# A graph layer in steps of 15 tiles instead of 16: second lookup in halves, sums of two spans in turn, slots on the full array

## The reference

```
msg = relu(x[src] + edge_attr)                  # (400000, 32)
agg = segment_sum(msg, dst, 12500)
h   = (1 + eps) * x + agg
y   = x + h @ W.T + b
out = (y - mean(y)) / sqrt(var(y) + 1e-5)       # over the 32 features
```

## Time and profile before

| what | value |
|---|---|
| median of 3 executions | 2076.12 us (2075.43 to 2078.41) |
| span of the profiled execution | 2071.9 us |
| PE busy | 2016.0 us, 97% |
| DVE busy | 1648.3 us, 80% |
| ACT busy | 1565.9 us, 76% |
| POOL busy | 1519.9 us, 73% |
| full steps | 195 |

### The profile page before, as it was taken

The page is one execution under the profiler, slowest core; times in us unless marked ns, Lnnn a source line. Parts: engine busy times, 40 slices in busy tenths (PEclk is TensorE's granted clock), DMA queues, the critical chain, the costliest instruction groups (busy, mean ns, idle before and its releaser), DMA issues. The chain is left out here.

```text
span 2071.9 us, 117127 instructions
## 1 busy us (share of the span) xinstructions
PE 2016.0 (97%) x46449; PEld 1922.5 (93%) x46449; DVE 1648.3 (80%) x4231; ACT 1565.9 (76%) x1616; POOL 1519.9 (73%) x1571
## 2 busy tenths in 40 slices
PE   4899999999999999999999999999999999999997
PEld 3899999999999999999999999999999999999994
DVE  7888778888888778888888877888888887788875
ACT  5777777777777777777777777777777777777773
POOL 6577777777777777777777777777777777777770
PEclk9999999999999999999999999999999999999998
DMA  6344454444444444544444444444444444444441
GB/s 163 84 111 113 113 114 114 112 110 109 110 111 112 112 113 114 114 110 110 110 110 110 114 112 113 112 114 109 110 110 110 111 113 113 111 114 114 110 110 34
DMA packets 236283, 228.68 MB, mean 110 GB/s; under 512 B 104218, under 2 KB 185556, under 8 KB 236062
## 3 DMA queue, kind: packets, MB, share of 16 engines
q1 hardware_dynamic: 186177, 202.59, 33.4%
q0 software_dynamic: 50080, 25.74, 13.3%
HBM read 225.43 MB, written 2.71 MB: 110 GB/s over the span
## 5 line engine op out<-in xcount | busy, mean ns | idle before, releaser
L541 POOL DMA_INDIRECT rows_all<-in_x,index x1565 | 1519.4, 971 | 502.8 <-issue 476.5
L1173 PE MATMUL found<-table,oh 128*128 128x128 bf16 x18720 | 1241.3, 225 | 11.5 <-issue 2.5
L1173 PEld LDWEIGHTS found<-table,oh 128*128 128x128 bf16 x18720 | 1168.1, 144 | 43.6 <-issue 20.0
L1012 ACT ACTIVATE oh<-keys,minus_lanes 128x1024 bf16<-128x1024 f16 x195 | 224.2, 1150 | 307.3 <-PE found L1173 294.5
L1154 PE MATMUL l<-xparts,oh 128*57 128x96 bf16 x18720 | 436.2, 207 | 0.9 <-ACT oh L1000 0.9
L1154 PEld LDWEIGHTS l<-xparts,oh 128*57 128x57 bf16 x18720 | 409.4, 108 | 14.0 <-issue 1.1
L993 ACT ACTIVATE oh<-slots,minus_lanes 128x1824 bf16<-128x1824 f16 x195 | 351.3, 1801 | 7.1 <-DMA slots<-slot_dram 7.1
L786 DVE COPY_PREDICATED rows_all<-mask,found 128x256 f32<-128x256 uint16 x780 | 343.1, 440 | 7.6 <-issue 1.4
L968 ACT CAST table<-l 128x768 bf16<-128x768 f32 x390 | 310.9, 798 | 39.7 <-PE l L1154 24.7
L1000 ACT ACTIVATE oh<-oh 128x1824 bf16<-128x1824 bf16 x195 | 335.7, 1721 | 0.0
L780 DVE TENSOR_TENSOR mask<-iota,side 128x32 f16<-128x32 f16 x195 | 37.5, 192 | 303.1 <-PE found L1173 291.0
(11 more groups left out here) (126 smaller groups left out, 906.5 us busy)
## 6 DMA issues: line engine op xcount, KB each, us to landing
slots<-slot_dram SPq DMA_DIRECT2D x195, 456.0 KB
msg<-in_edge SPq DMA_DIRECT2D x390, 128.0 KB
keys<-key_dram SPq DMA_DIRECT2D x195, 256.0 KB
rows_all<-in_x,index POOLq DMA_INDIRECT x1565
index<-in_src SPq DMA_DIRECT2D x195, 4.0 KB
key_dram<-key SPq DMA_DIRECT2D x195, 2.0 KB
slot_dram<-slot_row SPq DMA_DIRECT2D x195, 3.6 KB
oh<-in_x SPq DMA_DIRECT2D x3, 512.0 KB, 6.2
```

The source lines that it names most:

```text
L541: pool.indirect_dma_start(to, None, x, bass.IndirectOffsetOnAxis(indices[:, j:j + 1], 0)).then_inc(done, 16)
L1012: nc.scalar.activation(key_marks(b), by_edge(keys[:, four, :]), ACT.Square, bias=minus_lanes[:, b:b + 1]).then_inc(keys_squared, 1)
L1173: last = nc.tensor.matmul(found[:, t * FOUND:(t + 1) * FOUND], key_marks(b)[:, :, t], table[:, b, n * FOUND:(n + 1) * FOUND],  start=(b == ...
```

## The change

A step gets 15 tiles: 7 pooled, 8 looked up. With 5 tiles in the first batch there are then 208 full steps instead of 195. Further:

- The second lookup goes in halves of four tiles: all four blocks b for tiles 0 to 3 (with `fill_slots` behind b = 1 and `count_ranks` behind b = 3), then all four for tiles 4 to 7. The picks go in halves too, so there are eight of half the size: those of half 0 at the end of DVE's step s, those of half 1 at the start of step s+1. `mark_keys` of blocks 0 and 1 of row s+1 moves into DVE's step s, between picks.
- `sum_batch` moves from behind the first lookup to the end of PE's step, takes batch s instead of s-1, and takes one tile of each span in turn. `add_window` follows one step later instead of two.
- `fill_slots` loads 128 columns of weights instead of 32 and writes 128 partitions of PSUM, of which 32 are used.
- ACT's list becomes: `square_keys`, `mark_keys`, the two `fill_table`, `relu`, `copy_slots`, `square_slots`, `mark_slots`.
- The second and third turn of POOL's gathers wait for half 0 and for the whole second lookup of the row.

```diff
-    POOLED = 8
+    POOLED = 7
...
-    TURNS = [(0, 3), (3, 6), (6, POOLED)]
+    TURNS = [(0, 3), (3, 5), (5, POOLED)]
-    HEAD, FROM, TO = 4, -3, ROWS + 3
+    HEAD, FROM, TO = 4, -3, ROWS + 2
...
-        placed = sb("placed", [P, LOOK, BUCKETS], F16)
+        placed_store = sb("placed", [P, LOOK * BUCKETS + P - BUCKETS], F16)
...
-        slot_ps = ranks[0:BUCKETS, 384:384 + CAP]
+        slot_ps = ranks[:, 384:384 + CAP]
...
-                            pool.wait_ge(blocks_looked, (b - RING + 1) * KEYS + k * KEYS // 2)
+                            if k == 1:
+                                pool.wait_ge(half_looked, b - RING + 2)
+                            else:
+                                pool.wait_ge(blocks_looked, (b - RING + 2) * KEYS)
...
+            def pick(st, h, k):
+                if has(st, -h, ROWS):
+                    r, two, slot = st.s - h, slot_of(st, -h, 2), slot_of(st, 1 - h, RING)
+                    if k > 0:
+                        dve.wait_ge(picked[h], r * SIDE + k)
+                    elif h == 0:
+                        dve.wait_ge(half_looked, r + 1)
+                        dve.wait_ge(mask_ready, r + 1)
+                    else:
+                        dve.wait_ge(blocks_looked, (r + 1) * KEYS)
+                    dve.sem_inc(picks_started, 1)
+                    tiles = slice(h * HALF_TILES, (h + 1) * HALF_TILES)
...
             def step(st):
                 first, second = window_base(st, 0), window_base(st, 1)
+                pick(st, 1, 0)
+                mark_keys(st, 2)
+                pick(st, 1, 1)
+                count_before(st)
+                pick(st, 1, 2)
+                place_sources(st)
+                pick(st, 1, 3)
+                find_rank(st)
                 mark_sides(st)
                 add_rows(st)
                 give_key(st)
                 mark_buckets(st)
                 give_slots(st)
                 pair_buckets(st)
+                add_window(st, 0, first)
+                add_window(st, 1, second)
                 mark_batch(st)
+                mark_slots(st, 0)
+                pick(st, 0, 0)
+                mark_slots(st, 1)
+                pick(st, 0, 1)
+                mark_keys(st, 0, 1)
+                pick(st, 0, 2)
+                mark_keys(st, 1, 1)
+                pick(st, 0, 3)
...
                 for b in range(DVE_KEYS, KEYS):
                     square_keys(st, b)
+                mark_keys(st)
                 for h in range(2):
                     fill_table(st, h)
-                mark_keys(st)
                 relu(st)
+                copy_slots(st)
                 square_slots(st)
-                copy_slots(st)
                 mark_slots(st)
...
-            def look_in_table(st, b):
+            def look_in_table(st, h, b):
...
-                        wait_count(pe, picked_ready, r * SIDE)
+                        wait_count(pe, picked[h], r * SIDE)
...
-                    for t in range(LOOK):
+                    for t in range(h * HALF_TILES, (h + 1) * HALF_TILES):
...
-                    last.then_inc(blocks_looked, 1)
+                    if h == 1:
+                        last.then_inc(blocks_looked, 1)
+                    elif b == KEYS - 1:
+                        last.then_inc(half_looked, 1)

             def sum_tiles(n):
-                for g, tiles in enumerate(spans_of(n)):
-                    for j in tiles:
-                        last = nc.tensor.matmul(win_sums(g), relus[:, j, :], onehots[:, j, :], start=(j == tiles.start), stop=(j == tiles.stop - 1))
+                groups = spans_of(n)
+                for j in range(max(len(tiles) for tiles in groups)):
+                    for g, tiles in enumerate(groups):
+                        if j < len(tiles):
+                            last = nc.tensor.matmul(win_sums(g), relus[:, tiles[j], :], onehots[:, tiles[j], :], start=(j == 0), stop=(j == len(tiles) - 1))
...
-                        last = nc.tensor.matmul(slot_ps, placed[:, t, :], in_slot[:, t, :], start=(t == 0), stop=(t == LOOK - 1))
+                        last = nc.tensor.matmul(slot_ps, placed_store[:, t * BUCKETS:t * BUCKETS + P], in_slot[:, t, :], start=(t == 0), stop=(t == LOOK - 1))
...
-                sum_batch(st)
-                look_in_table(st, 0)
-                look_in_table(st, 1)
+                look_in_table(st, 0, 0)
+                look_in_table(st, 0, 1)
                 fill_slots(st)
-                look_in_table(st, 2)
+                look_in_table(st, 0, 2)
+                look_in_table(st, 0, 3)
                 count_ranks(st)
-                look_in_table(st, 3)
+                for b in range(KEYS):
+                    look_in_table(st, 1, b)
+                sum_batch(st)
```

More of the change, by code:

```diff
@@ L265, in gnn_kernel @@
         oh2_ready = sem("oh2_ready")
+        half_looked = sem("half_looked")
         blocks_looked = sem("blocks_looked")
         mask_ready = sem("mask_ready")
-        picked_ready = sem("picked_ready")
+        picked = [sem(f"picked{h}") for h in range(2)]
+        picks_started = sem("picks_started")
         src_loaded = [sem(f"src_loaded{h}") for h in range(2)]
@@ L677, in take_all_nodes @@
             def take_all_nodes():
-                for k in range(0, TILES // 2, 2):
+                for k in range(0, PAIRS, 2):
                     take_nodes(nc.vector.tensor_copy, dve, k)
@@ L759, in mark_slots, with mark_keys @@
                     nc.vector.tensor_scalar(oh1[:, j, :], slots[:, two, :], lanes[:, j:j + 1], None, ALU.is_equal).then_inc(oh1_ready, 1)
-            def mark_keys(st, b):
-                if has(st, 0, ROWS):
-                    r, four = st.s, slot_of(st, 0, RING)
+            def mark_keys(st, b, ahead=0):
+                if has(st, ahead, ROWS):
+                    r, four = st.s + ahead, slot_of(st, ahead, RING)
                     if b == 0:
@@ L767, in mark_keys @@
                             dve.wait_ge(sources_cast, 2)
-                        dve.wait_ge(keys_loaded[four], uses(st, 0) * 16 + 16)
+                        dve.wait_ge(keys_loaded[four], uses(st, ahead) * 16 + 16)
                     wait_count(dve, blocks_looked, (r - 1) * KEYS + (b + 1))
@@ L773, in mark_sides @@
             def mark_sides(st):
[L774 to L778, removed]
                 if has(st, 0, ROWS):
+                    wait_count(dve, picked[1], (st.s - 1) * SIDE)
                     nc.vector.tensor_tensor(mask[:, slot_of(st, 0, 2), :, :], count_up(iota, LOOK, SIDE), each(of_row(side, st.s), LOOK, SIDE),
                                             ALU.is_equal).then_inc(mask_ready, 1)
[L783 to L792, removed]
+            def pick(st, h, k):
[10 more added lines that the diff above has]
+                    tiles = slice(h * HALF_TILES, (h + 1) * HALF_TILES)
+                    to = rows[slot][:, POOLED * D:ROW].rearrange("p (t f) -> p t f", f=D)[:, tiles, :]
+                    nc.vector.copy_predicated(to, mask[:, two, tiles, k:k + 1].bitcast(U16).to_broadcast([P, HALF_TILES, D]),
+                                              found[:, 0:LOOK * FOUND].rearrange("p (t s f) -> p t s f", t=LOOK, s=SIDE)[:, tiles, k, :]).then_inc(picked[h], 1)
             def add_rows(st):
@@ L798, in add_rows @@
                     got = slice(0, (SHORT if isinstance(m, int) and m == 0 else TILES) * D)
-                    after_pick(st, SIDE - 1)
+                    for h in range(2):
+                        wait_count(dve, picked[h], m * SIDE)
                     dve.wait_ge(rows_gathered[slot], gathered(slot, use))
@@ L832, in step @@
                 first, second = window_base(st, 0), window_base(st, 1)
-                for b in range(EARLY_KEYS):
-                    mark_keys(st, b)
-                mark_sides(st)
[L836 to L847, removed]
+                pick(st, 1, 0)
[6 more added lines that the diff above has]
+                find_rank(st)
+                mark_sides(st)
                 add_rows(st)
@@ L1021, in step @@
                 if not st.inside and st.s == 0:
-                    for k in range(1, TILES // 2, 2):
+                    for k in range(1, PAIRS, 2):
                         take_nodes(nc.scalar.copy, act, k)
@@ L1093, in turn_x @@
                 pe.wait_ge(x_loaded, 16 * len(shares(NP)))
-                pe.wait_ge(picked_ready, st.s * SIDE)
+                for h in range(2):
+                    pe.wait_ge(picked[h], st.s * SIDE)
                 for k, (t0, n) in enumerate(ROUNDS_OUT):
@@ L1108, in turn_nodes @@
                 pe.wait_ge(late_taken, 1)
-                for k in range(TILES // 2):
+                for k in range(PAIRS):
                     if k >= 2:
                         pe.wait_ge(nodes_taken[k % 2], k // 2)
-                    for t in range(2):
-                        j = 2 * k + t
-                        at = j if j < POOLED else j - POOLED
```

(4 more changed lines are left out.)

45 lines of the change are left out of this document (25 added, 20 removed).

## The result

| | before | after |
|---|---|---|
| median of four runs, us | 2076.4 (2075.43 to 2078.41) | 2163.34 (2156.24 to 2168.63) |
| ratio | | 1.0418 [1.0405, 1.0431] |
| profiled execution: time, span, us | span 2071.9 | 2168.63, 2166.7 |
| step of the steady part, us | 10.15 | 9.875 |
| span outside the steps, us | 92.6 | 112.7 |

The account below looks back on a forecast made before the run. PE, busy 97%, was taken to bound the kernel before; after the change ACT's chain would hold PE at 9.80 us a step. 208 x 9.80 = 2038.4, + 92.6 + 4.2 = 2135 us, range 2062 to 2172.

Parts of the forecast that it names:

- Sums in turn: PE's window sums: alternating the two spans overlaps their matmuls, so the sums take 0.70 us instead of 1.25.
- Rival 3: PE's sums do not overlap, each matmul behind the one before: step 9.91 us, 2158 us in all; chance 5%.
- Slots on the full array: PE's eight slot matmuls: both changes of shape go and weight loads stay near today's pace, gaining 0.20 us a step.
- PE alone: PE's own list without waits for other engines: 2.86 us to the second lookup plus 6.54 behind it, step 9.40 us.
- ACT's chain: ACT's square_keys, mark_keys, first fill_table: PE's second lookup starts at 3.26 us instead of 2.86, a wait of 0.40 each step.
- DVE: the step that failed: DVE has 8.0 to 9.2 us of work in a 9.80 step; in_slot comes before fill_slots needs it at about 4.7.
- rival 4: Slower slot weight loads (0.25) or slow picks delaying in_slot (up to 0.2): step 10.0 to 10.05, 2177 to 2187 us; chance 13%.
- The sum: Whole step: 3.26 us to the second lookup plus 6.54 from there to the next step, 9.80 us.
- The start: Span outside the steady steps (start, first steps, output): kept at 92.6 us, as in the kernel before.

Follow-up runs that it names:

- the loads moved: The change, with DVE's two window-base loads moved from the start of its step to just ahead of the window sums: 2109.02 us, 1.0149 of the kernel before.
- PE's two edits alone: Kernel before with only sums in turn and slots on the full array, still 16 tiles, on a slower chip: 2928.15 us, 0.9667.
- all four edits: The change with mark_keys behind both fill_table, window-base loads late, PE's loop end behind the second lookup, sums cleared earlier: 2056.01 us (0.9896); slower chip 2937.18 (0.9694).

## Why the prediction was right in its sign and 28 us short

**Sums in turn: right.** Their 30 matmuls start within 0.57 us (16 x 0.036 = 0.57), after 1.02 for 32 before, and with the loop's end elsewhere the next part starts at G + 0.69, forecast 0.70. By the rule of the Trainium skill ("TensorE: Matmul & The Clock Gate", The mechanism) they would have taken 1.08 us of starts, from 30 x 0.036; measured are 0.57, so the rule does not hold for these two spans, which share their rows and differ in their columns. Rival 3 is out.

**Slots on the full array: right.** The eight starts take 0.24 (forecast 0.23), and with both changes of shape counted the slots cost 0.49 before and 0.30 after: a gain of 0.19, forecast 0.20.

**PE alone, 9.40: right for the list, wrong for its arrival.** With every cover restored the step is 9.383. But in the change PE was ready for the second lookup only at about G + 3.04, not G + 2.86, since the loop's jump back, which used to run while the matmuls of the second lookup were still at work, now has only the short sums ahead of it (its record starts at 1004.33, G + 0.29; before it was at 1008.95, 1.04 ahead of G): 0.18 us, a term that the sum did not have.

**ACT's chain: mechanism right, size too large.** Each term held (`table` starts at G + 2.32, its wait stands in 113 steps), but for the last: ACT to PE was taken as 0.12 from the earlier trace rows, at the start of the kernel, and is 0.03 here (first half of `table` ends at G + 3.12, PE starts at G + 3.15). The chain is 3.15, not 3.26, and with PE 0.18 late its wait is 0.12, not 0.40. Both together put the second lookup 0.11 earlier than forecast: by that alone the step would be 9.69.

**DVE: the step that failed.** The prediction said that "the moved marks and window sums cost the same as before", and let the work ahead of `in_slot` sum to 4.2. From the first pick to the end of `in_slot` it is 4.00 in the change and 4.01 with the loads moved, where `in_slot` is there at G + 4.23, in time: the sum of the durations was right to 0.2. What it left out is what does not count as busy: the two loads. Where they stand, at the head of the step, had not changed; what stands ahead of them had, short picks instead of the long marks that hid them before, and right behind them comes the pick that PE's list depends on. That put `in_slot` at G + 4.8 to 4.9 and cost 0.26 a step, about 54 us in 208. It is the wait of rival 4 (up to 0.2, measured 0.25 in the mean), with another cause.

**The sum.** 9.69 from ACT and 0.26 for the loads make 9.95; measured are 9.875. The means over all steps show the rest: the second lookup starts at G + 3.13, and from there to the next G it is 6.48 with the loads alone, where the forecast had 6.54; 3.13 + 6.48 + 0.26 = 9.87. Which matmuls are the 0.06 shorter stays open. Against the forecast 9.80 the step is +0.075, or +16 us: -0.13 from ACT's chain, -0.06 from the stretch behind it, +0.26 from the loads. That the forecast of the step came so close is thus partly luck, as two errors hid most of the third. The start added 20 us where the prediction kept 92.6: the window sums moved past ACT's clearing, a queue that it did not look at. And the median lies 3.4 below the span of the profiled run, not 4.2 above: -8. Together +28, 2163 for 2135, inside the range.

**Left open.** Whether POOL with eight gathers would hold a step of 9.38 was not tried. Nor were PE's two edits alone on a chip that feeds PE; with 3.3% on the other kind, and 0.65 us a step on paper, they may be worth more than the whole split.

## What to carry to other kernels

When instructions are moved, look also at what does not count as busy, value loads and jumps: where a queue of long instructions used to hide them, short ones or a wait may leave them on the path. A chain through another engine can be summed from its rows to a few hundredths, but the price of a hop should be taken from the same stretch of the kernel. And when a step's parts change places, follow the first two or three steps by themselves: what clears or prepares a buffer has to move along.

## What the runs showed of the hardware

- On two chips the kernel before took 2076 and 2078 us, on four others 3030 to 3087 us, with PE stopping for about 0.5 us inside a run of matmuls that wait for nothing. The sign of the change turned with the chip: 1.0418 on one kind, 0.9865 on the other. A loop body of four steps made the kernel before 4.2% slower there, and the version with all four edits 2.3% slower than before instead of 3.1% faster: the jump back, 0.21 us with a body of one, lasted 5.2 us (median of 27).
- Two f32 matmul spans on different columns of the array, taken in turn, overlap: 30 starts in 0.57 us.
- Loading two values for addresses on DVE took 0.72 us each on its sequencer, 1.4 in all; it cost nothing visible beneath marks of 0.49 to 0.80 us, and 0.26 us a step behind short picks.
- PE's jump back cost 0.18 to 0.19 us a step where only 0.6 us of matmuls stood ahead of it, and nothing visible behind 48 matmuls of the second lookup: the gap behind them is 0.16 us with the jump there and without it.
